# Slots dealt 14, 12, 12, 10 over four batches, and a re-ordered end of the program

## The reference, cut to what matters

```
xn  = layernorm(x)
q, k, v = xn Wq, xn Wkv                 # 32 heads of 16, 8 groups of k and v, each for 4 heads
ctx = softmax(causal(q k^T) / 4) v      # per batch and head
attn = ctx Wo + bo
top4 = the 4 best of 16 experts per token, by sigmoid(xn gate_w^T) + bias
ffn = sum over top4 of weight * (silu(xn Wg_e) * (xn Wu_e)) Wd_e  +  shared expert
out = x + attn + ffn
```

## Time and profile before

| | us |
|---|---|
| three runs, median (lowest to highest) | 502.7 (502.25 to 503.31) |
| the profiled execution's own time | 504.71 |
| its span, first to last instruction | 502.9 |

### The profile page before, as it was taken

The page is one execution under the profiler, slowest core; times in us unless marked ns, Lnnn a source line. Parts: engine busy times, 40 slices in busy tenths (PEclk is TensorE's granted clock), DMA queues, the critical chain, the costliest instruction groups (busy, mean ns, idle before and its releaser), DMA issues.

```text
span 502.9 us, 9687 instructions
## 1 busy us (share of the span) xinstructions
PE 454.6 (90%) x3074; PEld 348.6 (69%) x3074; DVE 360.7 (72%) x624; ACT 284.4 (57%) x435; POOL 192.5 (38%) x159
## 2 busy tenths in 40 slices
PE   5997999967998998999897999998999999999870
PEld 5776888845786786767675776686777857777630
DVE  7588874776787779849889887389789638775610
ACT  2732332504766776837787756486866637676510
POOL 2111649512444453324344444242344433353221
PEclk9998999988999998999999999998999999999995
DMA  6925853849947545886597778658864434443333
GB/s 254 410 64 144 182 197 90 290 158 216 273 119 174 121 73 145 227 266 117 92 293 201 246 184 139 193 116 180 239 133 87 85 66 73 76 85 46 49 55 42
DMA packets 31877, 77.92 MB, mean 155 GB/s; under 512 B 4048, under 2 KB 11728, under 8 KB 28912
## 3 DMA queue, kind: packets, MB, share of 16 engines
q0 software_dynamic: 11856, 27.27, 29.4%
q1 hardware_dynamic: 18864, 45.92, 28.7%
q10 hardware_dynamic: 1104, 4.06, 4.0%
HBM read 54.04 MB, written 23.07 MB: 153 GB/s over the span
## 4 chain that ended last, share of the span: by engine, by line
PE 59%; DMA 16%; DVE 10%; issue 5%; ACT 5%; ACTq 1%; DVEq 1%; POOL 1%; SPq 0%; POOLq 0%
PE psum L1209 34%; DMA out<-ysb,tab 8%; DMA out<-third_out,tab 4%; PE psum L1366 3%; PE psum L1172 3%; PE psum L1244 3%; PE psum L1354 3%; DMA xn_rows<-xn 2%; PE psum L1265 2%; PE psum L1249 2%; PE psum L1331 2%; PE psum L1232 2%; DVE wsplit L1012 2%; ACT wsplit L632 2%; DVE negm L997 1%
## 5 line engine op out<-in xcount | busy, mean ns | idle before, releaser
L1209 PE MATMUL psum<-wsplit,xgT 128*128 (+1 forms) x660 | 173.8, 415 | 11.1 <-DVE wsplit L1012 11.0
L1209 PEld LDWEIGHTS psum<-wsplit,xgT 128*128 128x128 f32 x660 | 126.0, 197 | 38.2 <-issue 12.9
L506 POOL DMA_INDIRECT out<-ysb,tab x32 | 55.5, 1734 | 127.1 <-ACT ysb L658 56.9
L1209 PE MATMUL psum<-wsplit,zT 128*128 (+1 forms) x330 | 92.7, 417 | 3.7 <-DVE zT L983 3.5
L1209 PEld LDWEIGHTS psum<-wsplit,zT 128*128 128x128 f32 x330 | 59.7, 192 | 16.8 <-issue 6.1
L997 DVE TENSOR_REDUCE negm<-psum 128x4 f32<-128x512 f32 x64 | 59.4, 954 | 12.6 <-PE psum L1249 12.2
L1065 DVE TENSOR_TENSOR plo<-xn,phi 128x1536 f16<-128x1536 f32 x32 | 56.2, 1756 | 11.1 <-ACT phi L711 10.1
L705 ACT ACTIVATE xn<-psum 128x1536 f32<-128x1536 f32 x32 | 46.3, 1448 | 22.4 <-PE psum L1339 14.0
L1007 DVE TENSOR_TENSOR xgT<-psum,xgT 128x512 fp32r<-128x512 f32 x47 | 32.3, 688 | 36.8 <-ACT xgT L628 36.0
L632 ACT ACTIVATE wsplit<-wraw (+1 forms) x48 | 48.9, 1054 | 5.8 <-SPq L376 5.8
L496 POOL DMA_INDIRECT xg<-xn_rows,tab x32 | 38.7, 1211 | 34.7 <-PE psum L1265 19.0
(11 more groups left out here) (192 smaller groups left out, 728.4 us busy)
## 6 DMA issues: line engine op xcount, KB each, us to landing
wraw<-wexp SPq DMA_DIRECT2D x17, 1024.0 KB, 6.8
wraw<-wexp SPq DMA_DIRECT2D x17, 512.0 KB, 4.5
q_parts<-stage SPq DMA_DIRECT2D x16, 192.0 KB
xn<-x SPq DMA_DIRECT2D x4, 512.0 KB, 5.3
xn_rows<-xn SPq DMA_DIRECT2D x8, 256.0 KB, 9.7
ctxs<-x SPq DMA_DIRECT2D x8, 256.0 KB, 4.7
out<-ysb SPq DMA_DIRECT2D x8, 256.0 KB, 3.3
out<-xn POOLq DMA_DIRECT2D x8, 256.0 KB, 4.2
```

The source lines that it names most:

```text
L506: nc.gpsimd.indirect_dma_start(out=out, out_offset=rows_of(s), in_=rows_out[s % 3], in_offset=None, compute_op=ALU.add).then_inc(y_out[par ...
L1209: last = MM(dst, lhs(a, k), split_weights(place, w, c), start=m == 0, stop=m == len(products) - 1)
```

## The change

Four edits. The slots are dealt 14, 12, 12, 10 over the batches: in the first batch groups 1 and 4 are beside pairs too, in the last one groups 5 and 7 are beside a single slot. On DVE `context` moves behind `gated` in a pair's second slot. At the end, three quarters of the last output product (the column blocks of groups 0 to 5) move ahead of the last group's weighted sums; the last block follows them. The wait for the last DMAs moves from POOL to SP.

```diff
-BESIDE = ((0, 1), (2,), (3,), (4, 5), (6,), (7, 8), (9,), (10, 11))
-SPS = sum(len(s) for s in BESIDE)
+MIDDLE = ((0, 1), (2,), (3,), (4, 5), (6,), (7, 8), (9,), (10, 11))
+BESIDE = (((0, 1), (2, 3), (4,), (5, 6), (7, 8), (9, 10), (11,), (12, 13)), MIDDLE, MIDDLE,
+          ((0, 1), (2,), (3,), (4, 5), (6,), (7,), (8,), (9,)))
+SLOTS = [sum(len(s) for s in beside) for beside in BESIDE]
+START = [sum(SLOTS[:b]) for b in range(B)]
...
-        WO = (PV, 2)
+        WO = (2, 3)
+        EARLY_K, LATE_K = range(KD - 1), range(KD - 1, KD)
...
@@ sync
             announce(1, NE - 1)
+            for par in range(2):
+                newest = NSLOT - 1 - (NSLOT - 1 - par) % 2
+                sp.wait_ge(y_out[par], 16 + 16 * (newest // 2 + 1))
+            sp.wait_ge(att_out, 16 * QT * B + 16)
...
@@ gpsimd
             for b in range(B):
                 sequence(b, b == B - 1)
-            pool.wait_ge(att_out, 16 * QT * B + 16)
...
@@ scalar, sequence
+                        if last and g == G - 1:
+                            for qt in range(QT):
+                                context_evac(b, qt, qt, slice(0, KD - 1))
-                        if j == BESIDE[g][0]:
+                        if j == BESIDE[b][g][0]:
                             high16(b, g)
...
                 if last:
                     y_evac(NSLOT - 1)
                     for qt in range(QT):
-                        context_evac(b, qt, qt)
+                        context_evac(b, qt, qt, slice(KD - 1, KD), 1)
...
@@ vector, sequence
-                        if not first and g:
-                            context(b, g - 1)
                         with_maxima = first and not (last and g >= 4)
...
                         if s < NSLOT:
                             gated(NT + s, j % 2)
+                        if not first and g:
+                            context(b, g - 1)
                         if s:
                             z_rest(s - 1)
...
@@ tensor, sequence
                 if last:
+                    pe.wait_ge(ctx_done, G * b + 6)
+                    pe.wait_ge(exp_done, G * (b + 1) + 1)
+                    for qt in range(QT):
+                        context_transpose(b, qt, qt, EARLY_K)
                     slot_down(NSLOT - 1, *expert.pop(NSLOT - 1))
-                if last:
-                    output_projection(b)
+                    for qt in range(QT):
+                        pe.wait_ge(ct_sb, QT * b + qt + 1)
+                        project_out(b, qt, WO[qt], EARLY_K)
+                    weighted(b, G - 1)
+                    pe.wait_ge(ctx_done, G * (b + 1))
+                    for qt in range(QT):
+                        context_transpose(b, qt, qt, LATE_K)
+                    for qt in range(QT):
+                        pe.wait_ge(ct_sb, QT * (b + 1) + qt + 1)
+                        project_out(b, qt, WO[qt], LATE_K)
```

More of the change, by code:

```diff
@@ L45 @@
 NSLOT = (TOPK * NTOK + (NE - TOPK) + NE * (P - 1)) // P
-BESIDE = ((0, 1), (2,), (3,), (4, 5), (6,), (7, 8), (9,), (10, 11))
-SPS = sum(len(s) for s in BESIDE)
-assert B * SPS == NSLOT + 1 and SPS % 2 == 0
+MIDDLE = ((0, 1), (2,), (3,), (4, 5), (6,), (7, 8), (9,), (10, 11))
[3 more added lines that the diff above has]
+START = [sum(SLOTS[:b]) for b in range(B)]
+assert sum(SLOTS) == NSLOT + 1 and all(n % 2 == 0 for n in SLOTS)
 NCOL = 1 + NSLOT
@@ L283, in beside_down @@
         def beside_down(b, g, j):
-            return j == BESIDE[g][0] and len(BESIDE[g]) == 2 and g % 4 != 3 and not (b and j == 0)
+            return j == BESIDE[b][g][0] and len(BESIDE[b][g]) == 2 and g % 4 != 3 and not (b and j == 0)
         def pack_half(eng, half, b):
@@ L503, in add_rows @@
                 pool.wait_ge(y_out[1 - par], 16 + (16 * ((s - 1) // 2 + 1) if s else 0))
-                if s > SPS and s % SPS in (1, 2):
-                    pool.wait_ge(att_out, 32 * (s // SPS) + (0 if s % SPS == 1 else 16))
+                b = sum(s >= first for first in START) - 1
+                if b and s - START[b] in (1, 2):
+                    pool.wait_ge(att_out, 32 * b + 16 * (s - START[b] - 1))
                 nc.gpsimd.indirect_dma_start(out=out, out_offset=rows_of(s), in_=rows_out[s % 3], in_offset=None,
@@ L711, in high16, with context_evac @@
                 S(phi[:, g % 2, :], pexp[:, g % 2, :], ACT.Copy).then_inc(hi16_done, 1)
-            def context_evac(b, qt, source):
-                    act.wait_ge(ct_ps, QT * b + qt + 1)
-                    S(ctxT[:, qt, :, :], bank(source).rearrange("p (k n) -> p k n", k=KD), ACT.Copy).then_inc(ct_sb, 1)
+            def context_evac(b, qt, source, chunks=slice(0, KD), late=0):
+                act.wait_ge(ct_ps, QT * (b + late) + qt + 1)
+                S(ctxT[:, qt, chunks, :], bank(source).rearrange("p (k n) -> p k n", k=KD)[:, chunks, :],
+                  ACT.Copy).then_inc(ct_sb, 1)
             def sequence(b, last, ahead):
                 for g in range(G):
-                    for j in BESIDE[g]:
-                        s, par = SPS * b + j, j % 2
+                    for j in BESIDE[b][g]:
+                        s, par = START[b] + j, j % 2
                         here, number = ahead
-                        if j == BESIDE[g][0]:
+                        if j == BESIDE[b][g][0]:
                             numerators(b, g)
-                        if j == BESIDE[g][-1] and (g == 3 or g == 7 and not last):
+                        if j == BESIDE[b][g][-1] and (g == 3 or g == 7 and not last):
                             minus_maxima(2 * b + (g // 4 + 1), 1 - g // 4)
@@ L1089, in sequence @@
                 for g in range(G):
-                    for j in BESIDE[g]:
-                        s, first = SPS * b + j, j == BESIDE[g][0]
+                    for j in BESIDE[b][g]:
+                        s, first = START[b] + j, j == BESIDE[b][g][0]
                         before, here, number = ahead
@@ L1381, in sequence @@
             def sequence(b, last, expert):
-                s0 = SPS * b
+                s0 = START[b]
                 for g in range(G):
-                    for j in BESIDE[g]:
-                        s, first, par = s0 + j, j == BESIDE[g][0], j % 2
+                    for j in BESIDE[b][g]:
+                        s, first, par = s0 + j, j == BESIDE[b][g][0], j % 2
                         if first:
                             scores(b, g, G * b + (min(g + 4, G) if last else g + 4))
-                        if j == BESIDE[g][-1] and (g == 3 or g == 7 and not last):
+                        if j == BESIDE[b][g][-1] and (g == 3 or g == 7 and not last):
                             maxima_transpose(G * b + (g + 5), 1 - g // 4)
```

35 lines of the change are left out of this document (14 added, 21 removed).

## The result

The change makes the kernel slower: 509.43 us (median of 4 runs, 509.07 to 512.07) beside 502.99 before (4 runs), a ratio of 1.0143, 95% interval 1.0112 to 1.0174. The forecast was 496.9, with 0.10 for slower. On another chip, later, the same kernel gave 1.0132 [1.0101, 1.0163]. The profiled execution took 509.54, its span is 507.7, against 504.71 and 502.9 before: 4.8 more. In the changed kernel the copy of a slot is L666, the slots' addition L515, the attention half's L522, the split L1024, the maxima L1009, `context` L1083 to L1088, the weighted sums L1366, the scores L1343 and the program's end L96.

A forecast was written before the change was run, and what follows sets the result against it. The prediction took POOL's chain of 13 steps over the last 71 us, then POOL's drain, as the bound. It summed 1.8 + 0 + 0 + 0 + 4.0 = 5.8 us, from 502.7 to 496.9, range 493.5 to 502.5.

The forecast's parts named there:

- The chain on POOL: Last batch's additions on POOL: start 9.62 us later, two additions (11.44) fewer, net 1.8 us earlier.
- A chain that ends later because it starts later than 419.2 + 9.6 = 428.9: Sign against the forecast, in POOL's last-batch additions: a start past 428.9 us that makes their end later.
- Four before, four after: zero: PE's waits of about 2 us for DVE's split weights: number unchanged, gain zero, one wait either way 3.7 us.
- more stalls on the weights: Rival: DVE's split late twice more, PE waits twice more at 3.7 us, 504.3 us; chance 0.08.
- It costs that `context` now delays the low part of the z product ...: nothing: Pair's second slot: `context` delays that part by 1.5 us, PE wants it 4.81 later at the least; cost zero.
- The product in two parts: Last output product at the program's end: reordering shortens a stretch no one waits for; zero, at most 1.3 us cost.
- The wait on SP: Program's end: POOL's drain starts 4.0 us earlier, keeps its 5.94 us, so the span ends 4.0 earlier.
- The rival that kept the drain in its place behind the landing: Rival at the program's end: no drain gain, only the chain's 1.8 us stays, 500.9 us; chance 0.20.
- 1.7 for half clock: After a PE wait of about 2 us, 3.4 us run at the 1.2 GHz level; half of that, 1.7, is lost.

The follow-up runs named there:

- context_alone: Kernel before with only `context` moved behind gating in a pair's second slot, slots as before; 501.71 us, ratio 0.9970.
- after_again: The changed kernel itself, unaltered, measured again on another chip; ratio 1.0132 to the kernel before.
- maxima_first_only: Changed kernel with one edit, the maxima ahead of the split in one-slot groups too; ratio 1.0081 to the kernel before.
- wait_alone: Kernel before with only the wait for the last DMAs moved from POOL to SP; 500.46 us, ratio 0.9961.
- late_slots_ctx: Changed kernel with slots 12, 12, 14, 10 and `context` ahead of the split in group 7 only; 497.69 us in ten runs, ratio 0.9883.
- slots_alone: Kernel before with only the new deal of slots 14, 12, 12, 10; 506.24 us, ratio 1.0058.

## Why the prediction was wrong

**The chain on POOL: right.** Eleven steps where there were 13, 59.1 against 71.7; the attention halves ready on DVE (493.5) before POOL takes them (496.95). "A chain that ends later because it starts later than 419.2 + 9.6 = 428.9" was named as what would prove the forecast wrong, and that is what happened: it starts at 438.10.

**The step that failed: "Four before, four after: zero".** The count was right for the waits it looked at: 119.74, 154.79, 205.91 and 259.60 stand where it put them, and the wait of 275.18 is gone as it said. But it looked at one kind of wait, the one largest in the rows of before. Five switches now fall into one-slot groups, where the maxima stand behind the split and the next turn's scores wait for them: 6.0 us in five waits, a kind that had 0.3 before. Only one of the five (slot 28's turn) was taken out of a turn with the maxima first; the other four (slots 11, 17, 20 and 29) stood in a pair's second slot, which has no maxima. The number of such turns is not all: the old deal had three of them (slots 18, 21 and 39). The kernel before waited 0.25 in the first of them, nothing in the second, and 1.23 in the third, behind the start of POOL's chain. In `context_alone`, where PE is held up less at the splits ahead of them, it is 0.89, 1.62 and 1.61. In these profiles, then, such a turn costs its wait only where PE isn't late itself. The run with the maxima moved prices them at 0.51%, 2.6 us. The rival "more stalls on the weights" (504.3, chance 0.08) had the right sign, but named the split, not what stands behind it.

**The second: "It costs that `context` now delays the low part of the z product ...: nothing".** One reader was named, the z product, and it had its cover. The other one was left out: PE's `weighted`, which refills the bank that `context` reads. In the other groups the refill comes a turn later; in group 7 it comes in the same turn. With the old deal the edit still gained 0.3% on balance: the turn of slot 11 has a switch in that place too, but PE was late there itself (0.89). With the new deal the turn of slot 25 has one, with nothing that holds PE up ahead of it, and the wait stands in all three profiles that have this deal and this order (3.63, 3.41 in `after_again`, 3.64 in `maxima_first_only`). The run without it prices it at 0.84%, 4.2 us, the pair on one chip at 0.94%, 4.7 us. That is most of the 7 us that appear only where the parts meet.

**The product in two parts: right**, zero measured as zero.

**The wait on SP: right mechanism, wrong size.** 4.0 forecast, 2.0 by the run alone, 1.5 by the trace. The argument that the 5.94 are a time of the drain's own holds; that they can begin at once doesn't: the drain started even before the last issue had ended, and took 10.1. The rival that kept the drain in its place behind the landing was right in that the end goes with the landing, but 4.2 behind it and not 6.1. The Trainium skill ("VectorE: DVE Perf Modes", section "The DRAIN you can't avoid") gives the DRAINs of the runtime's preamble and postamble as about 12 ns on all five engines. SP's at the end of this program took 13 ns and agrees. POOL's took 5,944 and 10,075, ACT's 370 and DVE's 730, so for these the rows decide; whether the page means these drains no run shows.

**What is left.** With both clashes removed the kernel is at 0.9987, the forecast was 0.9885: 5.1 us short. 2.0 of that is the drain's. The rest was not taken apart: PE is still idle 19.1 us from 112 us to the copy of slot 38, against 15.4 (18.1 in `wait_alone`) to that of slot 36 before, and POOL's additions run late in the second half (slot 28's came 14.0 us after its copy, before at most 9.8). `late_slots_ctx` reaches the forecast's time, but by another deal: that is no support for the forecast.

## What to carry to other kernels

When slots are dealt anew over a hand-written order, list for each turn that gets a switch every instruction that stands behind the switch's work, and who waits for it; a table of "waits of before" names only what is late now. When a read-out of PSUM moves back in a queue, price it for whoever refills that bank, not only for who needs the result. And try a combination as a whole: here four parts at -0.4 to +0.6% alone made +1.4% together, and one line about one group took 0.8% of it back.

## What the runs showed of the hardware

**The clock after a wait is not the same in each execution.** The forecast charged 1.7 for half clock with every wait of 2 us. The windows view of the 3.4 us behind the same three waits (2.37, 2.02, 2.00 us long), in the profiled execution of after and then in `after_again`, the same program:

```profile
119.74:123.14 3.40, 3.40 (x10) 2.73 (x11) 3.37 (x5) 0.15 (x1) 0.00 (x0) 0.64 0.95 153
154.79:158.19 3.40, 3.40 (x8) 2.72 (x9) 3.25 (x5) 0.60 (x1) 3.10 (x2) 0.51 0.78 217
205.91:209.31 3.40, 3.40 (x8) 2.72 (x9) 3.37 (x5) 0.62 (x2) 1.12 (x2) 0.52 0.90 129
```

```profile
118.31:121.71 3.40, 3.40 (x16) 2.72 (x17) 3.37 (x5) 0.49 (x2) 0.00 (x0) 1.00 1.10 192
152.38:155.78 3.40, 3.40 (x16) 2.83 (x17) 3.25 (x5) 0.94 (x2) 1.11 (x2) 1.00 0.84 172
202.04:205.44 3.40, 3.40 (x16) 2.78 (x17) 3.37 (x5) 0.93 (x3) 1.13 (x2) 1.00 0.86 129
```

After the same waits PE is granted about half in one execution, as in the earlier trace rows, and all of it in the other: 8 to 10 products of a kind against 16 in the same 3.4 us. Behind the two long waits that are new (3.63 and 2.78 us; 3.41 and 2.34 in `after_again`) it was about half in both executions: 0.51 and 0.50, and 0.54 and 0.54. So the idle time of PE can be compared between two profiles, and the time lost to the clock can't from one of each.

**POOL's drain** takes 5.94 us of its own also where all DMAs have long landed (5.78 in `slots_alone`), and 9.2 to 10.2 beside one just issued, in the profiles of the kernels that wait on SP. There, with nothing put ahead of it, it ended 4.2 to 4.3 us behind the landing each time.
